# A two-layer graph network on one core: moving the first stores and the first conversion, merging a packing pass, and splitting the exponential's clip off to ScalarE

## The reference, cut to what matters

```python
h = maximum(layernorm(x), 0)                        # x: 8192 x 64
mask = adj > 0                                      # adj: 8192 x 8192 int32, values 0 and 1
for i in (0, 1):                                    # two attention layers
    Wh = h @ W[i]
    e = leaky_relu(u + v.T + c, 0.2)                # u, v: one number a row, from Wh
    att = softmax(where(mask, e, -9e15), axis=1)
    h = 0.2 * x0 + 0.8 * elu(att @ Wh)
x = x + concat(x0, h1, h2) @ mlp_w + mlp_b          # x0 is the first h
h = maximum(layernorm(x), 0)
a = adj == 1
x = x + concat(a @ h / deg, h) @ weight + bias
```

## Time and profile before

| | |
|---|---|
| median of 3 runs | 1757.43 us (1756.73 to 1758.02) |
| the profiled execution's own time | 1757.3 us |
| its span, first to last instruction | 1755.5 us |
| busy share of the span | PE 87%, DVE 88%, ACT 72%, POOL 5% |
| mean granted TensorE clock | 0.975 |
| read from HBM, written | 325.45 MB, 27.33 MB |

### The profile page before, as it was taken

How to read it: one execution, slowest core, us unless ns; L and a number is a source line. 1 busy time by engine, 2 the same in 40 slices (tenths; PEclk the granted TensorE clock), 3 DMA queues, 4 the chain that set the end, 5 groups by cost and what they waited for, 6 DMA issues and landing times. The chain is left out here.

```text
span 1755.5 us, 50261 instructions
## 1 busy us (share of the span) xinstructions
PE 1532.0 (87%) x21779; PEld 1483.6 (85%) x21779; DVE 1539.7 (88%) x2544; ACT 1269.0 (72%) x1404; POOL 82.7 (5%) x116
## 2 busy tenths in 40 slices
PE   2268888888988888888779999999999999799998
PEld 2267778787878878787779999999999999799998
DVE  7799999999999999999788878879688788986665
ACT  4668888888979989888689999999999995000000
POOL 1100000101000010101010000000000000000000
PEclk9689999999999999999989999999999999999999
DMA  7998999999999999998121112122121211233231
GB/s 248 263 363 322 374 359 393 355 409 361 406 379 386 389 378 402 353 409 317 37 68 44 56 43 56 44 68 57 43 62 44 56 50 31 61 112 90 86 93 43
DMA packets 115389, 356.02 MB, mean 203 GB/s; under 512 B 9184, under 2 KB 17376, under 8 KB 115168
## 3 DMA queue, kind: packets, MB, share of 16 engines
q1 hardware_dynamic: 92192, 306.37, 46.9%
q0 software_dynamic: 8512, 27.33, 5.8%
q10 hardware_dynamic: 14464, 19.11, 3.0%
HBM read 325.45 MB, written 27.33 MB: 201 GB/s over the span
## 5 line engine op out<-in xcount | busy, mean ns | idle before, releaser
L461 ACT ACTIVATE region<-ub,bigv 128x1024 uint8<-128x1024 f32 x1024 | 1096.0, 1152 | 28.6 <-PE bank L1507 11.2
L1501 PE MATMUL bank<-wsplit,region 128*128 128x195 bf16 x8192 | 779.3, 248 | 46.2 <-DVE region L828 37.3
L1501 PEld LDWEIGHTS bank<-wsplit,region 128*128 128x128 fp8e3 x8192 | 687.1, 98 | 58.4 <-DVE region L828 41.3
L1507 PE MATMUL bank<-wsplit,region 128*128 128x130 f16 x8192 | 556.6, 221 | 63.4 <-DVE region L838 62.3
L1507 PEld LDWEIGHTS bank<-wsplit,region 128*128 128x128 fp8e3 x8192 | 499.0, 98 | 92.8 <-DVE region L838 92.7
L838 DVE SCALAR_TENSOR_TENSOR region<-region 128x512 uint32<-128x512 uint32 x512 | 338.4, 680 | 10.9 <-PE bank L1507 8.7
L828 DVE SCALAR_TENSOR_TENSOR region<-region 128x512 uint32<-128x512 uint32 x512 | 334.2, 681 | 10.8 <-ACT region L461 10.7
L850 DVE TENSOR_SCALAR region<-region 128x4096 uint8<-128x4096 int32 x128 | 292.0, 2281 | 9.6 <-DMA region<-in_adj 9.6
L1714 PE MATMUL bank<-wsplit,region 128*128 128x129 f16 x4096 | 243.5, 222 | 11.2 <-DVE region L1333 11.2
L1714 PEld LDWEIGHTS bank<-wsplit,region 128*128 128x128 fp8e3 x4096 | 241.4, 99 | 12.4 <-DVE region L1333 12.4
L1333 DVE TENSOR_SCALAR region<-region 128x512 uint32<-128x512 uint32 x256 | 100.2, 424 | 43.2 <-PE bank L1714 37.4
(11 more groups left out here) (192 smaller groups left out, 689.8 us busy)
## 6 DMA issues: line engine op xcount, KB each, us to landing
region<-in_adj SPq DMA_DIRECT2D x128, 2048.0 KB, 10.8
region<-codes_d SPq DMA_DIRECT2D x128, 256.0 KB, 2.7
codes_d<-region ACTq DMA_DIRECT2D x64, 256.0 KB, 6.4
ub<-u_d POOLq DMA_DIRECT2D x16, 512.0 KB, 6.1
hg<-h_d POOLq DMA_DIRECT2D x16, 256.0 KB, 6.2
stg<-m_d POOLq DMA_DIRECT2D x16, 256.0 KB, 5.0
region<-in_x SPq DMA_DIRECT2D x4, 512.0 KB, 6.8
h_d<-wsplit POOLq DMA_DIRECT2D x4, 512.0 KB, 4.4
```

Source lines behind the costliest of these rows:

```text
L461: last = nc.scalar.activation(sv[:, b, :], ub[G % 2][:, :], ACT.Relu, bias=bigv[l][:, t:t + 1], scale=BIG)
L1501: return nc.tensor.matmul(acc_on[it], columns(onb[U % NS], it, b), wsplit[:, c * TC + 2 * q + b, 0:WC], start=(c == 0 and q == 0 and b == ...
L1507: return nc.tensor.matmul(acc_off[it], columns(offb[U % NO], it, b), woff[:, c * TC + 2 * q + b, WO:WO + WF], start=(c == 0 and q == 0 and ...
```

## The change

Four things change.

1. The 8 stores of `m0` leave SP's queue and are issued by POOL, each after `store_u(k)` (and, for k = 0 and 1, after `load_u(k)`).
2. The first conversion, `convert(0, 0)`, stands ahead of the products; the second moves from k = 2 to k = 1, and the others of the start follow: the packing of step 0 is complete at k = 2, half tile 2 is converted at k = 3, `pack_pairs(1)` stands at k = 6 and `pack(1)` takes its old place ahead of `max_out`.
3. The two pair passes of 512 words become one of 1024 words that works in place in `code`; the last pass then reads both halves from there. The wait for the transposes of the step before moves from the first pass to the last.
4. For groups 0 to 6 of layer 0 VectorE's `exp_arg` is dropped. ScalarE takes relu(-att) and then exp(-that), with a semaphore wait on itself between the two; `attend` releases it. All later exponentials stay as they were (calls in them change only their argument).

```diff
-        STORES = {3: (0,), 4: (1, 2), 5: (3,), 6: (4, 5, 6, 7)}
@@ sync
-                    for k in STORES.get(m, ()):
-                        sp.wait_ge(mm_out, 3 * k + 3)
-                        sp.dma_start(dgrp(m0_d, k), m0[k]).then_inc(m0_st, 16)
@@ gpsimd
                     store_u(k)
                     if k < 2:
                         load_u(k)
+                    pool.wait_ge(mm_out, 3 * k + 3)
+                    pool.dma_start(dgrp(m0_d, k), m0[k]).then_inc(m0_st, 16)
@@ scalar, row_exp
                     act.wait_ge(mn_r, E + 1)
-                    nc.scalar.activation(ee, ee, ACT.Exp).then_inc(ex_r, 1)
+                    if E < NG - 1:
+                        nc.scalar.activation(ee, att[:, :, :], ACT.Relu, scale=-1.0).then_inc(clip, 1)
+                        act.wait_ge(clip, E + 1)
+                    nc.scalar.activation(ee, ee, ACT.Exp, scale=-1.0 if E < NG - 1 else 1.0).then_inc(ex_r, 1)
@@ vector
-                cq = [code[:, :, 256 * q:256 * (q + 1)].bitcast(U32) for q in range(QC)]
+                cq = w32(code.rearrange("p t j -> p (t j)")).rearrange("p (t h s w) -> p t h s w", t=IT, h=2, s=2)
                 def pack_pairs(n):
                     dve.wait_ge(coded, 2 * n + 2)
+                    nc.vector.scalar_tensor_tensor(cq[:, :, :, 0, :], cq[:, :, :, 1, :], 2, cq[:, :, :, 0, :], ALU.logical_shift_left,
+                                                   ALU.bitwise_or).then_inc(pairs_r, 1)
+
+                def pack(n):
+                    dve.wait_ge(pairs_r, n + 1)
                     if n > 0:
                         dve.wait_ge(tp_done, n)
-                        dve.wait_ge(packed_r, n)
-                    nc.vector.scalar_tensor_tensor(pk, cq[1], 2, cq[0], ALU.logical_shift_left, ALU.bitwise_or).then_inc(pairs_r, 1)
-                    nc.vector.scalar_tensor_tensor(cq[2], cq[3], 2, cq[2], ALU.logical_shift_left, ALU.bitwise_or).then_inc(pairs_r, 1)
-
-                def pack(n):
-                    dve.wait_ge(pairs_r, 2 * n + 2)
-                    nc.vector.scalar_tensor_tensor(pk, cq[2], 4, pk, ALU.logical_shift_left, ALU.bitwise_or).then_inc(packed_r, 1)
+                    nc.vector.scalar_tensor_tensor(pk, cq[:, :, 1, 0, :], 4, cq[:, :, 0, 0, :], ALU.logical_shift_left,
+                                                   ALU.bitwise_or).then_inc(packed_r, 1)
@@ attend
-                    ec.mark(nc.vector.tensor_tensor(att[:, :, :], av[:, :, 0:C], wide(rd[:, :]), ALU.mult))
+                    last = nc.vector.tensor_tensor(att[:, :, :], av[:, :, 0:C], wide(rd[:, :]), ALU.mult)
+                    if E < NG - 1:
+                        last.then_inc(mn_r, 1)
+                    else:
+                        ec.mark(last)
@@ VectorE's order in the start
                 low0(3)
+                convert(0, 0)
                 for k in range(NG):
                     for r in range(3):
                         columns_0(k, r)
                     if k > 0:
                         largest_0(k - 1)
                     if k == 1:
-                        convert(0, 0)
+                        convert(0, 1)
                     if k == 2:
-                        convert(0, 1)
                         pack_pairs(0)
+                        pack(0)
                     if k == 3:
-                        pack(0)
-                    if k == 4:
                         convert(1, 0)
                     if k == 5:
                         convert(1, 1)
+                    if k == 6:
+                        pack_pairs(1)
                 biased_0()
                 largest_0(NG - 1)
                 max_parts(0)
                 max_row(1)
-                pack_pairs(1)
+                pack(1)
                 max_out(1, hmx[:, 1, :])
                 scales(0)
-                pack(1)
                 convert(2, 0)
@@ the steps of the first pass
-                    if g > 0 and r == 2:
-                        exp_arg(g - 1)
```

More of the change, by code:

```diff
@@ L244, in gnn_program @@
         red, ech, mn_r, ex_r = sem("sums_added"), sem("row_chain"), sem("exp_arg"), sem("exp_done")
+        clip = sem("exp_arg_clipped")
         hg_in = [sem(f"h0_loaded{i}") for i in range(2)]
@@ L1243, in _ @@
                         if r == 3:
-                            exp_arg(g - 1)
+                            exp_arg(NG + g - 1)
                         if r == 4:
@@ L1291, in _ @@
                         if r == 2:
-                            attend(g - 1)
+                            attend(NG + g - 1)
                         if r == 4:
@@ L1364, in _ @@
                 pick_half(4)
-                attend(7)
+                attend(NG + 7)
                 normal_2(6)
-                exp_arg(7)
+                exp_arg(NG + 7)
                 high_3(6)
```

## The result

The changed kernel takes 1752.99 us (median of 10 runs, 1750.55 to 1755.63) against 1757.88 for the kernel before, a ratio of 0.997 with a 95% interval of 0.9961 to 0.998. It is faster by 4.9 us. I had forecast 12.1 us and a range of 1738.0 to 1751.5: the direction was right, the size was less than half of it, and the time lies outside the range.

A forecast was written before the change was run, and what follows sets the result against it. VectorE was taken to bound the first pass, with transfers close behind and setting the pace until 98 us. Start 6.0, packing 3.7 and clip 2.4 sum to 12.1 off 1757.3, giving 1745.2 us, range 1738 to 1751.5.

The forecast's parts named there:

- the sentence on POOL's stores: Start, m0 stores on POOL: the last lands at about 81 us, before VectorE's first off mask needs it, so hidden.
- the bytes are the same: Start, transfers from half tile 3 to half tile 7: same bytes, started 6.4 us earlier, so finished 6.4 earlier.
- parts 3 and 4: VectorE's merged packing pass, 3.7 us over 61 steps, and its dropped clip, 2.4 us over 7 groups.
- The issue at 67.6: POOL's queue in the start: its m0 and column stores would all be issued by about 67.6 us.
- Half tile 7 at 91.5: Start, adjacency load: half tile 7 would land at 91.5 us, 6.4 earlier, and be wanted at 85.3.
- The start's 6.0: Start, moved stores and reordered conversions: VectorE gains 6.0 us, the supply bound of 6.4 less 0.4.
- The walk without waits (12.9): Start: VectorE's timeline if it waited for no transfer, first off mask at 80.0; upper bound 12.9 us.
- rival A: Start gains all: with stores and half tiles on separate queues VectorE waits for nothing; 1738.3 us, chance 0.18.
- That the transfers would allow both: Past 110 us: transfer supply has 6% slack against under 1% shortening per group, so nothing was charged.
- C: Start: slow POOL issues make the last m0 store land at 103.8, delaying the first off mask; 1762.1 us, chance 0.04.
- D: Gains come and are eaten, by a store landing at 95.5 to 102.5 or otherwise; within 3.5 us of 1757, chance 0.05.
- The rule on descriptors: POOL's stores: GpSimd cannot write descriptors while VectorE runs a two-port mode, so stores moved there would come late.

The follow-up runs named there:

- experiment 5: Changed kernel with layer 0's column stores of k = 2 to 7 written as 128 pieces of 32 bytes, not 512 of 8 (wrong row values, timing only): 1741.66 us.
- experiment 2: Changed kernel with POOL's column stores of k = 2 to 7 issued only after all 8 m0 stores have landed: 1745.41 us.
- experiment 7: Kernel before, with none of the change's four parts, column stores of k = 2 to 7 spread over group 0: 1749.14 us.
- experiment 6: Changed kernel with column stores of k = 2 to 7 spread over steps 2 to 7 of group 0, group 1's row load behind the m0 stores: 1739.07 us.
- experiment 9: Changed kernel with column stores spread as in experiment 6, but the m0 stores back on SP's queue: 1738.36 us.
- experiment 3: Kernel before with only the merged packing pass and the clip on ScalarE; start and stores as before: 1751.3 us.

## Why the prediction was wrong

**The step that failed** is the sentence on POOL's stores: "With the 13.1 us that the quickest of SP's last four stores took to land [...], the last one lands at about 81, beside 80.0 wanted without any wait and 86 wanted in my sum: hidden." It landed at 94.1, and VectorE stood 13.3 us at the first off mask. The row that I leaned on gave 13.1, 14.5 and 27.4, and I took the quickest, although I had seen the slow flow in the earlier trace rows and had the last store issued right behind six column stores in the midst of it. I never asked what the slow flow came from; I wrote that the bytes are the same and so the end moves with the start. It does not: the slow flow belongs to the column stores, not to the bytes. Experiment 5 shows it by their pieces, experiment 2 by their place, experiment 7 on the kernel before. Had this step alone been right, half tile 7, landed at 94.0, would have been the bound: by my estimate the start would have gained 98.15 - 94.0 = 4.1, for a time of some 1747 with the 5.8 of parts 3 and 4.

**The issue at 67.6** was 71.4. (The terms as I wrote them add up to 67.1.) I left the first row load where it was, at 43.49. With half tile 3 now flowing, the column store ahead of it lands later and the load is issued at 48.82; the next one waits till 61.12, not 55.5.

**Half tile 7 at 91.5**: 94.0, against 97.9 before. Half tile 3 was issued at 39.49, 5.9 us earlier and not 6.4, and of this 3.9 came through to half tile 7, as the slow flow grew from 14 us to about 22 us, at some 200 GB/s.

**The start's 6.0** was -1.15. The walk without waits (12.9) was nearly right: the changed kernel reached the off mask at 80.8 against 80.0, so 12.1 earlier, and experiment 6 began it at 81.33. The items that I gave for it (9.6 and 1.5 of waits, 0.9 of idle time) make only 12.0; the walk had the rest without a row. Experiments 6 and 9 gain nearly all of it: 1758.05 - 1739.07 = 19.0, which was the sum for rival A.

**Parts 3 and 4 (3.7 and 2.4)**: together 5.6 to 7.0 in experiment 3, with a pitch of 1.13 for 1.14. That the transfers would allow both held too: 0.6 us of waits.

**The rivals.** C named the place, the wait and the queue behind it, and I gave it 0.04 with a landing at 103.8. The store landed at 94.1, between my forecast and C, and C's reason, issues of 1.99 each, was met by two issues only. I had given D, "the gains come and are eaten", 0.05 from a landing of 95.5 on, and left the stretch from 86 to 95.5 to no case at all, though my two landings of 13.1 and 27.4 span it. A landing at 94.1 makes 1757.3 + 1.15 - 6.1 = 1752.4 by my own sum, 0.3 from the profiled execution's 1752.64, and the range ended at 1751.5 because this case was missing. A asked for a cause of the slow flow and found the wrong one, the blocked queue; experiment 7 shows the blockage as an effect.

**The rule on descriptors** (the Trainium skill, "SBUF — State Buffer", the box on DVE blocking DMA): beside conversions at 49.59 and 64.96, two of POOL's 16 issues of stores took 2.64 and 2.80 us, the others 0.54 to 0.76, and each of the two ended 0.1 to 0.3 us after the conversion did. The trace agrees with the rule; that the conversion runs in a two-port mode no row shows. Its price was some 4 us of issue time, while the landing of the last store took 9.6 us more than I had put in. Experiments 6 and 9, one queue against the other, cannot be told apart.

## What to carry to other kernels

Before a transfer is moved in time, find out what makes the neighbouring ones slow: six stores of 4 KB each, cut into 8-byte pieces, cost the kernel before 8.9 us (experiment 7), and the cost lands on other transfers, microseconds after the stores are issued. When several landings of the same kind differ by a factor of two, a wait that rests on them belongs to the slowest one until the reason is known. Put such stores where the consumer is slower than the transfers, and move a DMA from one queue to another only with a reason that the trace shows.

## What the runs showed of the hardware that I had not expected

Stores of 512 pieces of 8 bytes slow the transfers of the other queues. Six in a row gave some 15 us at mostly less than 220 GB/s where about 400 is had, beginning 4 to 6 us after the first was issued (experiment 2). One by itself, issued at 146.55 in experiment 6, gave some 3 us at 233 to 352 GB/s, beginning 5 to 6 us after its issue and ahead of its landing at 153.9. In 128 pieces of 32 bytes the same stores left no trace (experiment 5). The Trainium skill, "DMA: Bandwidth & Descriptors", the table of its section "Specifications", has transfers under 512 B do a read-modify-write and fall short of line rate. The runs add that the loss is borne by other transfers too, and that 32 bytes, also far under 512, were harmless here. Whether the write to memory itself is what blocks was not tried, nor whether the same 8-byte stores from SP's queue would slow the others as much: in every run POOL issued them.
